# Routing of a mixture-of-experts layer moved into the state-space block before it, chunk by chunk

## What is computed

```
h  = layernorm(layernorm(x)) * g + b
x1 = x + layernorm(x) + mamba(h)      # W_in, 4-tap causal convolution, silu, scan with 16 states
                                      # over 512 channels, gate silu(z), W_out
n  = layernorm(x1)                    # no gain or bias
logits = n @ Wg + bg                  # 8 experts; the best two, weights by softmax over the two
mixed  = sum over the two of weight * (relu(n @ W1[e] + b1[e]) @ W2[e] + b2[e])
out = x1 + layernorm(mixed + n) * gamma + beta
```

## Time and profile before

| | us |
|---|---|
| three runs | 2862.16, 2864.79, 2869.3 |
| median | 2864.79 |
| profiled execution, its own time | 2865.76 |
| its span | 2864.0 |
| state-space block, first scan to last scan | 61.5 to 1850.3 |
| routing stage, up to the first tile on PE | 1869 to 2134.9 |
| tile stage | 2134.9 to 2692.9 |
| combine | 2692.9 to 2864.0 |

### The profile page before, as it was taken

How to read it: one execution, slowest core, us unless ns; L and a number is a source line. 1 busy time by engine, 2 the same in 40 slices (tenths; PEclk the granted TensorE clock), 3 DMA queues, 4 the chain that set the end, 5 groups by cost and what they waited for, 6 DMA issues and landing times. The chain is left out here.

```text
span 2864.0 us, 36830 instructions
## 1 busy us (share of the span) xinstructions
PE 2081.1 (73%) x9614; PEld 1465.6 (51%) x9615; DVE 2111.3 (74%) x2737; ACT 1447.5 (51%) x2613; POOL 2102.2 (73%) x1378
## 2 busy tenths in 40 slices
PE   6886877877878778778788686644419999999500
PEld 2554555555655555555556455533416666666400
DVE  3999999999999999999999999833313333333389
ACT  5566666665665676666666665323313333333200
POOL 2999998998999999999999999717742222222377
PEclk9989989989889889898898898655559999999855
DMA  4133131241330431322413304063332222222265
GB/s 133 51 126 103 40 133 66 84 133 40 108 134 18 131 103 40 133 68 82 133 41 108 126 17 132 1 226 134 113 122 65 65 63 66 63 66 63 73 211 193
DMA packets 150819, 272.14 MB, mean 95 GB/s; under 512 B 16769, under 2 KB 106369, under 8 KB 150434
## 3 DMA queue, kind: packets, MB, share of 16 engines
q1 hardware_dynamic: 123138, 216.06, 23.3%
q0 software_dynamic: 12624, 34.62, 3.3%
q10 hardware_dynamic: 14928, 19.92, 2.0%
HBM read 216.14 MB, written 54.41 MB: 94 GB/s over the span
## 5 line engine op out<-in xcount | busy, mean ns | idle before, releaser
L475 POOL TENSOR_TENSOR dbu<-du,bb 128x1024 f32<-128x1024 f32 x512 | 1202.8, 2365 | 89.8 <-DVE ps_a L360 83.9
L617 ACT ACTIVATE ps_a<-dl,a_neg 128x512 f32<-128x512 f32 x1024 | 682.0, 684 | 279.5 <-DVE ss L360 148.2
L765 PE MATMUL ps_y<-ident,wd 128*128 128x128 f32 x2816 | 442.7, 309 | 127.4 <-DVE wd L373 126.2
L765 PEld LDWEIGHTS ps_y<-ident,wd 128*128 128x128 f32 x2816 | 383.2, 162 | 257.5 <-DVE wd L373 172.8
L1360 POOL DMA_INDIRECT eo_scratch<-tiles,idx x135 | 129.4, 959 | 439.6 <-ACT tiles L1463 426.7
L360 DVE TENSOR_TENSOR_SCAN ps_a<-ps_a,carry,dbu 128x512 f32<-128x512 f32 x352 | 434.2, 1281 | 6.9 <-ACT ps_a L617 6.9
L373 DVE TENSOR_TENSOR wd<-ps_a,cc 128x1024 f32<-128x1024 f32 (+1 forms) x384 | 429.0, 1118 | 0.0
L360 DVE TENSOR_TENSOR_SCAN ps_a<-ps_a,dbu 128x512 f32<-128x512 f32 x352 | 412.8, 1218 | 17.5 <-ACT ps_a L617 17.1
L492 POOL TENSOR_TENSOR wp<-ss,cc 128x1024 f32<-128x1024 f32 (+1 forms) x192 | 384.6, 2003 | 2.3 <-DVE ss L360 2.3
L1248 DVE TENSOR_TENSOR hidden<-e_ps_h,b1b 128x512 f32<-128x512 f32 x135 | 93.4, 692 | 256.2 <-PE e_ps_h L1531 256.2
L1531 PE MATMUL e_ps_h<-w,tiles 128*128 x540 | 255.6, 596 | 0.3 <-ACT tiles L1449 0.3
(11 more groups left out here) (151 smaller groups left out, 3014.3 us busy)
## 6 DMA issues: line engine op xcount, KB each, us to landing
bb<-b_scratch SPq DMA_DIRECT2D x128, 512.0 KB, 3.7
cc<-b_scratch SPq DMA_DIRECT2D x128, 512.0 KB, 5.5
xt<-xs_scratch SPq DMA_DIRECT2D x135, 129.0 KB, 2.1
r_x<-x_scratch SPq DMA_DIRECT2D x32, 512.0 KB, 6.0
big<-eo_scratch SPq DMA_DIRECT2D x32, 512.0 KB, 5.4
xb<-in_L_attn_x_dram SPq DMA_DIRECT2D x16, 512.0 KB, 6.3
hx<-in_L_attn_x_dram SPq DMA_DIRECT2D x16, 512.0 KB, 6.1
x_scratch<-hx SPq DMA_DIRECT2D x16, 512.0 KB, 2.9
```

Source lines behind the costliest of these rows:

```text
L475: pool.tensor_tensor(dbu[:, k % NBU], du[:, g % 2, :].unsqueeze(1).broadcast_to([P, 2, CH]), bb[:, 2 * m:2 * m + 2, :], ALU.mult).then_inc ...
L617: act.activation(ps_a[:, bank(k), :], dl[:, g, :], ACT.Exp, scale=a_neg[:, g, n:n + 1]).then_inc(exp_done, 1)
L765: ins = pe.matmul(ps_y[:, i, :], wd[:, s % NWD, h, i * P:(i + 1) * P], ident[:], start=False, stop=False, is_transpose=True, skip_group_ch ...
```

## The change

The second layer norm, the router, the choice of the two experts, the ranks and the scatter of rows leave the expert block and are done for each chunk in the state-space block, one to two chunks behind the scan. The experts' weights are still loaded in the expert block. Details:

- **Order of work.** `STEADY` has new steps, a number of parts and a lag for each entry, and three new kinds: `turnx` (turn n), `logit` and `rank`. Chunk offset -2 means that a chunk's entry stands in the second chunk after it. The way back of y no longer has a buffer of its own (`yg`); it is written into `zt`.
- **DVE** takes over `factors` (four small instructions), and gets `stats_x1` (10 instructions) and `route_step` (21) for each chunk. The steps are set between the scans at the offsets of `ROUTE`: chunk q's stand at steps 18 to 40 of chunk q+2.
- **ACT** makes the power as Ln and Exp (`inv_std`), n (`normalise_x1`, straight from `hx`), and `row_meta`, and empties `turnx`. `stage` has one buffer for both choices: the second choice's weight is written when the first choice's rows have landed.
- **POOL** loses `factors` and gets 8 scatters for each chunk.
- **SP** also loads Wg and bg at the start, and load_again comes ahead of load_x.
- **After the last scan** the routing of the last two chunks is still to be done, in the same order of steps.
- **Expert block.** The routing stage is gone; tables, padding and weight loads remain. In the combine ACT makes n again from x1 and the kept factors (`again`), and its loops are written out.

```diff
+        STEADY = [("h", 0, 1, 0, 1, 5), ("h", 1, 1, 0, 1, 7), ("x", 0, 1, 2, 1, 6), ("turnx", 0, -2, 4, 1, 4),
+                  ("turnx", 1, -2, 4, 1, 5), ("back", 3, -1, 6, 1, 6), ("x", 1, 1, 6, 2, 6), ("x", 2, 1, 9, 2, 7),
+                  ("conv", 0, 1, 8, 4, 8), ("logit", 0, -2, 15, 1, 2), ("x", 3, 1, 17, 1, 3),
+                  ("conv", 1, 1, 19, 2, 5), ("conv", 2, 1, 20, 4, 6), ("conv", 3, 1, 22, 4, 6),
+                  ("out", 0, -1, 25, 4, 14), ("rank", 0, -2, 30, 1, 1), ("dbc", 0, 1, 31, 4, 7),
+                  ("back", 0, 0, 35, 1, 4), ("dt", 0, 1, 35, 1, 7), ("out", 1, -1, 35, 2, 9), ("z", 0, 1, 40, 2, 5),
+                  ("back", 1, 0, 44, 1, 3), ("dt", 1, 1, 44, 1, 5), ("z", 1, 1, 45, 2, 7), ("z", 2, 1, 50, 1, 6),
+                  ("dt", 2, 1, 51, 1, 3), ("z", 3, 1, 52, 1, 7), ("back", 2, 0, 60, 1, 8), ("dt", 3, 1, 62, 1, 3)]
...
+        ADD_DT = ((41, 0), (48, 1), (58, 2), (65, 3))
+        RESIDUAL = ((30, 0), (41, 1))
+        STATS = (47, 47, 50, 54)
+        INV_STD = (55, 55)
+        STATS_X1 = (43, 47, 49, 51)
+        INV_STD_X1 = (53, 53)
+        XN = (56, 57)
+        ROUTE = (82, 84, 84, 85, 86, 87, 88, 89, 90, 91, 92, 92, 96, 97, 98, 100, 101, 103, 103, 103, 104)
+        EXP_W = 99
+        IDS_0 = 107
+        IDS_1 = 115
+        SCATTER = ((54, 0, 0), (55, 0, 1), (55, 0, 2), (55, 0, 3), (58, 1, 0), (58, 1, 1), (59, 1, 2), (59, 1, 3))
+        GATE = 4
...
+            def factors_a(q):
+                dve.wait_ge(ln_step, 3 * q + 2)
+                dve.tensor_scalar(pw[:, 0, :], mv[:, :, 1], 1.0 + EPS, EPS * EPS, ALU.mult, ALU.add)
+                dve.tensor_scalar(pw[:, 1, :], mv[:, :, 1], EPS, None, ALU.add).then_inc(ln_step, 1)
+            def factors_b(q):
...
+                dve.tensor_scalar(sc[:, r, :], rr[:, r, 1, :], 1.0, None, ALU.add)
+                dve.scalar_tensor_tensor(nb[:, r], mv[:, :, 0].unsqueeze(1).broadcast_to([P, 2, NT]), -1.0, rr[:, r],
+                                         ALU.mult, ALU.mult).then_inc(prm, 1)
...
+            def route_step(q, j):
...
+                if j == 0:
+                    dve.wait_ge(proj_full, full("logit", 0, q))
+                    ins = dve.tensor_tensor(lg[:], proj("logit", 0, q)[:, 0:NT * E].rearrange("p (i e) -> p i e", e=E),
+                                            bgb[:].unsqueeze(1).broadcast_to([P, NT, E]), ALU.add)
+                elif j in (1, 6):
+                    ins = dve.tensor_reduce(mx[:, j // 6, :], lg[:], AX.X, ALU.max)
+                elif j in (2, 7):
+                    ins = dve.tensor_tensor(eq[:], lg[:], mx[:, j // 6, :].unsqueeze(2).broadcast_to([P, NT, E]),
+                                            ALU.is_equal)
+                elif j in (3, 8):
+                    ins = dve.tensor_tensor_scan(cn[:].rearrange(flat), first[:].rearrange(flat),
+                                                 eq[:].rearrange(flat), 0.0, ALU.mult, ALU.add)
+                elif j in (4, 9):
+                    ins = dve.scalar_tensor_tensor(sel[:, j // 6], cn[:], 1.0, eq[:], ALU.is_equal, ALU.mult)
+                elif j == 5:
+                    ins = dve.scalar_tensor_tensor(lg[:], sel[:, 0], -3e38, lg[:], ALU.mult, ALU.add)
+                elif j == 10:
+                    ins = dve.tensor_tensor(both[:], sel[:, 0], sel[:, 1], ALU.add)
+                elif j == 11:
+                    ins = dve.tensor_tensor(ex[:], mx[:, 1, :], mx[:, 0, :], ALU.subtract)
+                elif j == 12:
+                    dve.wait_ge(proj_full, full("rank", 0, q))
+                    ins = dve.tensor_tensor(slot[:], proj("rank", 0, q)[:, 0:NT * E].rearrange("p (i e) -> p i e", e=E),
+                                            base[:], ALU.add)
+                elif j == 13:
+                    ins = dve.tensor_reduce(tot[:], both[:].rearrange("p i e -> p e i"), AX.X, ALU.add)
+                elif j == 14:
+                    ins = dve.tensor_tensor(seen[:], seen[:], tot[:], ALU.add)
+                elif j == 15:
+                    ins = dve.tensor_tensor(pick[:], sel[:], slot[:].unsqueeze(1).broadcast_to([P, 2, NT, E]), ALU.mult)
+                elif j == 16:
+                    ins = dve.tensor_reduce(slf[:], pick[:], AX.X, ALU.add)
+                elif j == 17:
+                    dve.wait_ge(scat, 16 * 2 * NT * q)
+                    ins = dve.tensor_copy(sli[:], slf[:])
+                elif j == 18:
+                    dve.wait_ge(e_done, q + 1)
+                    ins = dve.tensor_scalar(den[:], ex[:], 1.0, None, ALU.add)
+                elif j == 19:
+                    ins = dve.reciprocal(wt[:, 0, :], den[:])
+                else:
+                    ins = dve.tensor_tensor(wt[:, 1, :], wt[:, 0, :], ex[:], ALU.mult)
...
+            def scatter(q, k, i):
+                pool.wait_ge(*routed(q, 17))
+                pool.wait_ge(meta, 2 * q + k + 1)
+                pool.indirect_dma_start(
+                    out=xs_dram, out_offset=bass.IndirectOffsetOnAxis(ap=sli[:, k, i:i + 1], axis=0),
+                    in_=stage[:, i, :], in_offset=None).then_inc(scat, 16)
...
+            def normalise_x1(q, tiles):
+                act.wait_ge(lnr_step, 4 * q + 4)
+                if q > 0:
+                    act.wait_ge(scat, 16 * 2 * NT * q)
+                    act.wait_ge(proj_full, full("turnx", 1, q - 1))
+                for i in tiles:
+                    ins = act.activation(stage[:, i, 0:D], hx[:, i, :], ACT.Identity, bias=x_ln[:, 1, q, i:i + 1],
+                                         scale=x_ln[:, 0, q, i:i + 1])
...
+            def row_meta(q, k):
+                act.wait_ge(*routed(q, 19 + k))
+                act.wait_ge(scat, 16 * NT * (2 * q + k))
+                act.copy(stage[:, :, D], wt[:, k, :])
+                act.copy(stage[:, :, D + 1], idf[:, k, q * NT:(q + 1) * NT]).then_inc(meta, 1)
...
+            def again(c, q):
+                par = q % 2
+                wait_slot(act, x1_in[q], c, XR, q)
+                wait(act, summed, 2, c, -2)
+                for i in range(NT):
+                    ins = act.activation(xn[:, par, i, :], x1[:, q, i, :], ACT.Identity,
+                                         bias=x_ln[:, 1, c, i:i + 1], scale=x_ln[:, 0, c, i:i + 1])
+                ins.then_inc(xn_done, 1)
```

More of the change, by code:

```diff
@@ L166, in mamba_block @@
[L166 to L173, removed]
-        SKIP_Y = 5
[L175 to L179, removed]
@@ L428, in _ @@
-            weigh(LAST, 5)
-            gate(LAST)
-            residual(NC - 1, 0)
-            residual(NC - 1, 1)
+            for at in range(STEPS):
+                c, s = divmod(at, SG)
+                t, n = divmod(at, N)
+                if c < NC:
+                    scan(c, s // N, n)
+                if n == 0 and 0 < t <= LAST + 1:
+                    weigh(t - 1, 5)
+                if n >= 3 and n % 3 == 0 and t <= LAST:
+                    weigh(t, n // 3 - 1)
+                if n == GATE and 0 < t <= LAST + 1:
+                    gate(t - 1)
+                for offset, g in ADD_DT:
+                    q = due(at, offset, 1)
+                    if q is not None:
+                        add_dt(q, g)
+                for offset, j in RESIDUAL:
+                    q = due(at, offset, -1)
+                    if q is not None:
+                        residual(q, j)
+                for j, offset in enumerate(STATS):
+                    q = due(at, offset, 2)
+                    if q is not None:
+                        (stats_a, stats_b, factors_a, factors_b)[j](q)
+                for j, offset in enumerate(STATS_X1):
+                    q = due(at, offset, -1)
+                    if q is not None:
+                        stats_x1(q, j)
+                for j, offset in enumerate(ROUTE):
+                    q = due(at, offset, -1)
+                    if q is not None:
+                        route_step(q, j)
@@ L1376, in combine @@
                 inv_std(c, par, c_stat, c_rs)
-            chunks(pool, combine)
+            chunks(combine)
         @block.scalar
         def _(act):
-            act.wait_ge(counted, 1)
-            def stage_rows(j, q):
-                par, c = q % 2, j * GC + q
-                if q == 0:
-                    wait(act, step, KR, j, KR)
-                wait(act, kept, 1, c, 1)
-                wait_slot(act, scat[par], c, 2, par, per=16 * SC, more=-1)
-                for k in range(2):
-                    act.copy(stage[:, par, k, :, 0:D], at(xn, c))
-                act.copy(stage[:, par, :, :, D], wt[:, :, q * NT:(q + 1) * NT])
-                act.copy(stage[:, par, :, :, D + 1], idf[:, :, bass.ds(c * NT, NT)]).then_inc(staged, 1)
             def load_experts():
```

730 lines of the change are left out of this document (331 added, 399 removed).

## The result

The changed kernel takes **2946.05 us** (median; 2945.6 to 2951.47) beside 2866.78 us of the kernel before on the same chip: ratio 1.0283, 95% interval [1.0264, 1.0302]. It is slower. The forecast was 2842, and the measured time lies above the whole range. The profiled execution has a span of 2944.7 us, 80.7 more than the 2864.0 of before. Where they come from is read in the windows by stage (columns: window, length, then busy us and instructions of PE, PEld, DVE, ACT and POOL, then TensorE's granted clock, DMA share, GB/s); they answer to the earlier trace rows.

What follows compares the result with a forecast made beforehand. DVE and POOL were taken as nearly full in the scans, DVE setting the pace. Start +2, scans +154, tail +44, front of the expert block -224, combine 0 gave -24 against 2865.8: 2842 us, range 2725 to 2915.

Steps and rivals of the forecast that it cites:

- The lock: Scans: new DVE instructions reading two SBUF tensors stand still until POOL's running instruction ends; 9.8 us per chunk.
- the lock bites more: Rival, DVE between scans: two-input instructions meet POOL at random or worse, single-input ones held too; 127.5 per chunk, 2908; chance 0.22.
- The race behind a scan: Scans: DVE instructions behind an odd scan start before POOL's, those behind an even one lose 1.0 to 1.6 us.
- What DVE and POOL get: Scans: work per chunk with the routing moved in, DVE 111.0 us without the lock, POOL 113.1 us.
- POOL's floor: Scans: POOL needs 113.1 us per chunk with 8 scatters added, the least a chunk can take.
- small reads slip through: Rival, scans: small DVE reads are not held, POOL's 113.1 is the bound, period 115.5, 2740 us; chance 0.22.
- The order of work: Scans: GATE and RESIDUAL move later, DVE's waits for PE mostly go; 6 us of waits per chunk become 2.
- The start: Before the first scan: dbc and dt ahead of z save 4 us, table loads and z's copies cost; +2 us.
- The tail: Last scan to block end: two chunks' routing is left, 62.5 us instead of 18.7; +44 us.
- the front of the expert block: Block start to first tile: routing stage goes, weight load stays, 42 us (bounds 37, 52) instead of 266; -224 us.
- The combine: Combine: x1 passes through ACT before DVE adds n, arrives just in time, loop jumps go; 0 us (bounds -6, +26).
- the path that the rival gave: Combine bound by its loads: x1 through ACT comes 2 us late per chunk, +26 us, 2868; chance 0.08.

Runs made afterwards that it cites:

- The run with both burdens: Kernel before, with 12 small two-input tensor_tensor on DVE and 8 scatters on POOL added in each of 14 chunks: 3048.10 us, ratio 1.0631.
- the version without held forms: Changed kernel with statistics and route rewritten without waiting forms, slot cast on ACT, z first, exact ties not broken: 2731.06 us, ratio 0.9523 to the kernel before.

## Why the prediction was wrong

- **The step that failed is "The lock", in its size.** The mechanism was right: a small DVE instruction that reads two SBUF tensors stands still beside a POOL that multiplies, whatever its size. The term said 9.8 us per chunk and the trace shows 17.7. By the term's own parts (measured for forecast): the route steps 9.4 for 8.3, the two `scalar_tensor_tensor` of the statistics (L450, L429) 5.7 for 1.5, and `tensor_scalar` 2.5 for nothing. The second part is the largest miss. It took "the rest of POOL's instruction" as the most that one can wait, from the earlier trace rows; L450 outlasts it in 12 of 15 places, up to 7.3 us. All holds of that kind add 73 us, 5.2 a chunk; without them the two-input instructions are at 9.9, beside the forecast of 9.8. The run with both burdens shows that scatters in POOL's queue make such holds. In the changed kernel itself the scatters were not taken away, and four holds of 4.9 us (L470) stand half a chunk from them.
- **From the term to the scans.** 7.9 us in 14 chunks are 111. Of these 25 came back as DVE's other waits (95 us before, forecast 95 - 14 x 3.9 = 40, measured 16) and 8 as its own new work (22.2 - 17.7 = 4.5 us a chunk instead of 5.1). Net 78, the whole difference of the scans.
- **Its list was too short.** `tensor_scalar` of 4 elements (L421, L447, L428) was counted as free; in the changed kernel it is held for 35 us. The rival "the lock bites more" named it, and its period of 127.5 is near the measured 111.8 + 231.8 / 14 = 128.4. It had 0.22, and it was the case that came, with luck in the number: it priced the two-input instructions at 11.2 us a chunk (15.2 measured) and had DVE's other waits too high. It still fell 38 us short, 12 of them in the scans and the rest in start, combine and front.
- **The race behind a scan** came out in part. The forecast had instructions behind an odd scan slip by and those behind an even one lose. L473 slips by behind both kinds (steps 22 and 27), L467 at step 25 is held for 1.5 us in all 14 chunks, and L470 at step 21 slips by in ten chunks and is held for 4.9 us in four.
- **What DVE and POOL get** was right: the 113.1 us of POOL's floor are what the version without held forms shows (113.9). That its 2731 us lie within 9 of the 2740 of "small reads slip through" is in part luck: its scans are 21 us shorter than that rival had them, its combine 11 longer.
- **The order of work**: waits for PE before gate and residual fell from 28.3 and 21.3 us to 8.3 and none, and DVE's waits from 95 to 16 us. A DVE that is always late waits less in any case, but in the last version, where the holds are gone, the two are at 8.4 us and none as well, so that step was right.
- **The start**: +12.5 instead of +2. The parts were listed (two table loads, z's copies) and mis-sized; z's four projections at their place behind dt hold ACT's silu(z) back to 69.99, and the first exponential starts at 73.2. With z first the first scan begins at 62.5.
- **The tail** (+44.1 against +44) and **the front of the expert block** (46.8 against 42, within 37 to 52): right by their own steps. From the last scan's end chunk 15's rows may be written at 31.4 us (forecast 32) and its first scatter starts at 47.9. The steps as listed add up to 61.2 us and the sum took 62.5; the trace has 62.8. The route steps in the tail, where POOL runs no tensor instruction, take 0.16 to 0.23 us.
- **The combine**: +10.6, within -6 to +26. The waits name the path that the rival gave, which was priced at 26:

```profile
ACT r_xn L1508 <- DMA r_x<-x_scratch: 108.9, 12, 18.5
DVE big L1372 <- ACT r_xn L1508: 21.1, 6, 3.8
```

No run took the combine apart; that x1 through ACT is the cause is read from this trace alone.

One reading of the page was off without any effect on the sum: DVE is at 9 tenths in 25 of 40 slices and POOL in 22, not both in 26.

## What to carry to other kernels

Before small VectorE instructions are moved beside a GpSimd that multiplies SBUF tensors, list them by form, not by size. In these runs two SBUF tensors, copies, casts and `tensor_scalar` waited for what GpSimd ran, and at times for several of its instructions (up to 7.3 us). Reduces, max, reciprocal, a `tensor_scalar` of a single column, and the steps with one operand in PSUM cost their own 0.15 to 0.2 us. Rewriting pays in full only when all such forms near a busy GpSimd are rewritten, since the wait goes to the next one that is held: 74 us removed in one place gave 21, all of them gave 215. A forecast needs the longest run of GpSimd instructions without a pause, and whether the change makes it longer.

## What the runs showed of the hardware

- A 4-element DVE instruction took 7.28 us beside four POOL instructions in a row. In the kernel before, holds longer than one product (2.36 us) occur only with scatters in POOL's queue (8 of 168, maximum 5.13 us; without scatters 1.96).
- A `tensor_tensor` of one element is held (median 1.15 us), a `tensor_scalar` of one element is not (maximum 0.154). A `tensor_scalar` of 32 elements is held with a constant and with a per-partition scalar, one of 8 with a per-partition scalar (maximum 1.5 for the three), one of 4 with constants (maximum 2.9, L447).
- A step with one operand in PSUM is not held: 0.179 to 0.192 us beside a POOL that is busy 97% of the time (L469, L478 of the last version).
- The scatter's issue on POOL takes 0.954 to 1.234 us, median 0.966, in the changed kernel, beside a DVE that is busy 99% of the time.
